# Products with rounded halves for the output and the state in an adaLN block, and bn_aggr in its first layer norm

## The chip, the cores and the metric

The kernel runs on one core of one Trainium2 chip. Its time is the device time of one execution in microseconds, here the median of three runs. Engines are called PE (TensorE), DVE (VectorE), ACT (ScalarE), POOL (GpSimd) and SP (SyncE, which issues the DMAs). Each works through its own list of instructions in order; semaphores tie the lists together.

## The reference

The input x is 16 batches of 512 positions with 256 channels. A block with adaptive layer norm is computed: a state space model and a gated mix, each behind a modulated layer norm and a gate.

```python
sa, ca, ga, sb, cb, gb = split((silu(c) @ wmod))      # per batch, 256 each
h = layernorm(x) * (1 + ca) + sa
u, gate = split(h @ W_in.T)
b_t = u @ W_state.T
dt = min(softplus(u @ W_dt.T + b_dt), 10)
decay = exp(-dt * rate)                                # rate from A_log
state[t] = decay[t] * state[t-1] + (1 - decay[t]) * b_t[t]    # 128 states
y = state @ W_C.T
z = y * silu(gate) + h * D
x = x + ga * (z @ W_out.T)
h = layernorm(x) * (1 + cb) + sb
xr, xk = mixes of h with h of the position before
out = x + gb * (sigmoid(xr @ W_r.T) * (relu(xk @ W_k.T)**2 @ W_v.T))
```

## The kernel before

A batch is worked in the layout channels x positions: two halves of 128 channels (partitions) by 512 positions. An fp32 array of this shape is 128x512 per half. The 16 batches run through a pipeline written out by hand: in step s each engine does parts of four batches, a = s, b = s-1, c = s-2 and d = s-3. Batch a gets its first layer norm (LN1) applied and transposed; b goes through the state space model (h, dt, b_t, gate, scan, y, z, W_out, x1); c through the second layer norm (LN2) and the mixes; d through W_k, W_r, W_v and the output. The order within a step is the order in the source of each engine's block; nothing reorders it. The four PSUM slots (of two banks each) are shared by several results, which sets more waits.

Most products are done in three passes. A value and its weight are each split into a rounded half of type fp32r (`_hi`) and the rest (`_lo` = value - hi, also fp32r). PE then adds hi x hi, hi x weight-lo and lo x weight-hi in PSUM: `half(out, w, at, x, c)` issues two products of 128x512 for half c of the input. ACT makes the hi parts (`nc.scalar.copy`), POOL the lo parts (`low_part`, L665). So it is for h, xk, xr and k. Two products are done in plain fp32: that of z with W_out (`half(o_out, w_late, OUT, z, ...)`, L207, four products a batch) and that of the state with W_C (L320, two a batch).

What touches the change, in the order of a step on each engine:

- PE: xk_hi of d, halves 0 and 1; dt, b_t of b from h_hi and xk_lo of d between them; dt from h_lo (ends dt, `dt_ps`); transposes of x1 of c (L290, `t2_ps`); xr_hi and the gate; y from the state of b (L320, `y_ps`); xr_lo half 0; half of the transposes of xn2 of c (L214); xr_lo half 1 (`r_ps`); the other transposes (`t3_ps`); k_hi; transposes of xn1 of a (L214, `t1_ps`); k_lo half 0; z half 0; k_lo half 1; z half 1 (`o_ps`).
- ACT: xk_hi, h, h_hi, xr_hi; the exp of dt (L427), relu, ln, decay; xn1 of a, tiles 0 and 1 (L446); k_hi (L452), silu (L456), k_act (L462); the tanh r_gate (L465, waits for `r_ps`); the four prevs of c (L392, wait for `t3_ps`), then the next step.
- DVE: the scan (L587, `state_ok`); xn2 (L526); y x silu (L599) and z (L604); xk, xr, xr, xk of c (L550, after `prev_ok`); LN1 statistics of batch a+2 (L489, bn_stats); rv (L624); LN1 mean and variance of a+2 (L496 to L505, five small instructions on 128x4); x2 of d (L631); x1 of b (L637, waits for `o_ps`); xn1 of a+1, tiles 2 and 3 (L520); the clip of dt (L644); LN2 statistics from `t2_ps` and its mean and variance; the drive (L658), which the scan follows.
- POOL: xk_lo, h_lo, xr_lo half 0; rstd of LN2 (L698); xr_lo half 1; LN1's rstd (L672, a pow) and shift (L674); k_lo.

x1 of batch b is made at the end of step s from PSUM, and PE transposes it in the next step. In the first two steps PE has idle stretches and runs products with zeros (`keep_warm`).

Of the kernel before, what the change touches and what calls it, by code (L numbers as in the profile page):

```python
# [26 lines left out]
def adaln_block(nc, x_tok_d, x_ch_d, w_d, wmod_d, c_d, cols_d, ident_d, out_d):  # L27
# [6 lines left out]
    with ExitStack() as ctx:  # L34
# [20 lines left out]
        wl_hi = sb("wl_hi", [P, CH, 3 * C], F32R)  # L55
        wl_lo = sb("wl_lo", [P, CH, 3 * C], F32R)
# [22 lines left out]
        mv1 = sb("mv1", [P, 2, 5, TT])  # L79
# [48 lines left out]
        wl_hi_ok, wl_lo_ok = sem("wl_hi_ok"), sem("wl_lo_ok")  # L128
# [74 lines left out]
        def _(pe):  # L203
# [43 lines left out]
            for s in STEPS:  # L247
                a, b, c, d = s, s - 1, s - 2, s - 3
                if live(d):
                    if d == 0:  # L250
# [4 lines left out]
                    half(k_out, wl_hi, MIX_K, xk_hi, 0, first=True)
                    half(k_out, wl_lo, MIX_K, xk_hi, 0)
                if live(d):
                    pe.wait_ge(xkhi_ok[1], d + 1)
# [50 lines left out]
                if live(b):  # L309
# [64 lines left out]
                if live(b):  # L374
# [4 lines left out]
        def _(act):  # L379
# [15 lines left out]
            for s in STEPS:  # L395
                a, b, c, d = s, s - 1, s - 2, s - 3
                if live(d):
# [68 lines left out]
                if live(c):  # L466
# [6 lines left out]
                    previous(REC, 0, c).then_inc(prev_ok[0], 1)  # L473
                    before(act, xr_ok[1], c)
# [5 lines left out]
        def _(dve):  # L480
# [11 lines left out]
            def mean_variance(st, mv, st_ok, halves_ok, spread_ok, mv_ok, k, negative=False):  # L492
# [6 lines left out]
                if negative:  # L499
                    nc.vector.scalar_tensor_tensor(mv[:, 0, :], mv[:, 2, :], 0.5, st[:, :, 1], ALU.mult, ALU.subtract)  # L500
                else:
                    nc.vector.scalar_tensor_tensor(mv[:, 0, :], mv[:, 2, :], -0.5, st[:, :, 1], ALU.mult, ALU.add)
# [79 lines left out]
            for s in STEPS:  # L582
                a, b, c, d = s, s - 1, s - 2, s - 3
                if live(b):
                    dve.wait_ge(drive_ok, b + 1)
                    before(dve, y_ps, b)
# [9 lines left out]
                if live(b):  # L596
# [5 lines left out]
                    for i in range(CH):  # L602
                        before(dve, o_ps, b)
# [57 lines left out]
        def _(pool):  # L661
# [5 lines left out]
            def ln1_scale(k):  # L667
# [81 lines left out]
```

## Time and profile before

| | |
|---|---|
| median of 3 runs | 390.41 us (390.02 to 390.94) |
| the profiled execution's own time | 390.1 us |
| its span in the trace | 388.3 us |
| PE, DVE, ACT, POOL busy | 95%, 82%, 74%, 52% of the span |

The profile is one execution. A line of a view in order of time has the start in us from the start of the span, the time it lasts, engine, source line, operation, output and inputs, and the count of instructions that were merged to it. A full fp32 product shows as two records. The start of a product on PE is when it was taken up, which can be a little before the one ahead has streamed through.

### The profile page before, as it was taken

The numbers are of one execution on the slowest core, as the hardware profiler recorded it, in microseconds if no ns is written. First come the engines' busy times: TensorE is split into PE (matmuls) and PEld (weight loads), VectorE is DVE, ScalarE is ACT, GpSimd is POOL, SyncE is SP. The second block draws the span as 40 slices with busy tenths as digits, with TensorE's granted clock in tenths as the row PEclk, the third lists the DMA queues.
The fourth block names the chain that finished last, engine by engine and source line by source line (L and its number), as shares of the span: only waits on it lengthen the run. The fifth ranks groups of instructions, "written<-read, shape, count | busy, mean of one in ns | idle before, by whom it ended". The sixth has DMA issues, their size and how long they took to land.

```text
span 388.3 us, 5293 instructions
## 1 busy us (share of the span) xinstructions
PE 369.3 (95%) x1624; PEld 265.3 (68%) x1627; DVE 317.1 (82%) x653; ACT 288.6 (74%) x375; POOL 201.8 (52%) x198
## 2 busy tenths in 40 slices
PE   8998899999999999999999999999999999999773
PEld 4766487676777677676767767676767767676651
DVE  3787987989889797988979798888979787768552
ACT  4467678687887878689687868888787878967471
POOL 2053355666364556656454566645455663635552
PEclk9999999999999999999999999999999999999998
DMA  8921111130403131040313113040302020000111
GB/s 283 394 77 54 54 57 54 56 110 0 164 0 108 55 104 60 12 152 0 118 47 108 56 56 107 3 159 3 111 0 87 24 92 17 23 32 0 57 54 54
DMA packets 18604, 29.13 MB, mean 75 GB/s; under 512 B 1168, under 2 KB 9616, under 8 KB 18448
## 3 DMA queue, kind: packets, MB, share of 16 engines
q1 hardware_dynamic: 18144, 28.71, 21.4%
q8 instruction: 13, 0.21, 0.2%
q10 hardware_dynamic: 432, 0.09, 0.1%
q14 instruction: 15, 0.12, 0.1%
HBM read 20.40 MB, written 8.39 MB: 74 GB/s over the span
## 4 chain that ended last, share of the span: by engine, by line
issue 49%; POOL 37%; PE 7%; DVE 3%; ACT 2%; POOLq 1%; DVEq 0%; ACTq 0%
POOL xr_lo L665 10%; POOL xk_lo L665 10%; POOL k_lo L665 6%; POOL h_lo L665 5%; POOL rstd L672 3%; PE slot L207 2%; PE slot L228 2%; PE slot L221 1%; DVE stats L489 1%; PE slot L320 1%; POOLq L24 1%; POOL prev L703 1%; PE slot L214 1%; ACT prev L392 1%; DVE state L587 1%
## 5 line engine op out<-in xcount | busy, mean ns | idle before, releaser
L665 POOL TENSOR_TENSOR xk_lo<-xk,xk_hi 128x512 fp32r<-128x512 f32 x32 | 40.9, 1279 | 52.7 <-ACT xk_hi L400 47.1
L207 PE MATMUL slot<-z,w_in 128*128 128x512 f32 x128 | 59.8, 592 | 0.0
L698 POOL TENSOR_TENSOR rstd<-mv,half_neg 128x4 f32<-128x4 f32 x16 | 16.1, 1007 | 76.5 <-DVE mv L505 76.5
L665 POOL TENSOR_TENSOR k_lo<-k_act,k_hi 128x512 fp32r<-128x512 f32 x32 | 40.6, 1291 | 20.7 <-ACT k_act L462 20.7
L392 ACT ACTIVATE prev<-slot,mod,mix_prev 128x512 f32<-128x512 f32 x64 | 44.5, 784 | 2.8 <-PE slot L214 2.8
L207 PE MATMUL slot<-h_hi,wf_hi 128*128 128x512 f32 x128 | 46.0, 400 | 0.4 <-ACT h_hi L415 0.4
L207 PE MATMUL slot<-h_hi,wf_lo 128*128 128x512 f32 x128 | 45.1, 393 | 0.0
L665 POOL TENSOR_TENSOR h_lo<-h,h_hi 128x512 fp32r<-128x512 f32 x30 | 38.3, 1298 | 9.6 <-ACT h_hi L415 9.6
L427 ACT ACTIVATE dt<-slot,cols 128x512 f32<-128x512 f32 x16 | 11.0, 688 | 41.5 <-PE slot L207 41.5
L665 POOL TENSOR_TENSOR xr_lo<-xr,xr_hi 128x512 fp32r<-128x512 f32 x32 | 41.5, 1299 | 0.0
L550 DVE SCALAR_TENSOR_TENSOR xk<-slot,mix_new,prev 128x512 f32<-128x512 f32 x32 | 23.9, 747 | 18.8 <-issue 18.8
L214 PE MATMUL slot<-ident,xn 128*128 128x128 f32 x256 | 35.7, 273 | 2.8 <-DVE xn L526 2.1
L207 PE MATMUL slot<-h_lo,wf_hi 128*128 128x512 f32 x128 | 37.4, 395 | 0.0
L214 PEld LDWEIGHTS slot<-ident,xn 128*128 128x128 f32 x256 | 30.4, 140 | 10.1 <-DVE xn L526 2.8
L207 PEld LDWEIGHTS slot<-z,w_in 128*128 128x128 f32 x128 | 24.0, 189 | 18.8 <-issue 16.3
L320 PE MATMUL slot<-state,w_in 128*128 128x512 f32 x64 | 30.2, 594 | 2.5 <-DVE state L587 2.5
L526 DVE TENSOR_SCALAR xn<-slot,mv,rstd 128x256 f32<-128x256 f32 x64 | 30.1, 534 | 1.1 <-POOL rstd L698 1.1
L599 DVE TENSOR_TENSOR slot<-silu,slot 128x1024 f32<-128x1024 f32 x16 | 19.7, 1229 | 13.5 <-PE slot L320 13.5
L465 ACT ACTIVATE r_gate<-slot 128x1024 f32<-128x1024 f32 x16 | 16.4, 1028 | 18.6 <-PE slot L207 18.6
L207 PEld LDWEIGHTS slot<-h_hi,wf_hi 128*128 128x128 f32 x128 | 24.0, 188 | 6.7 <-issue 0.9
L207 PE MATMUL slot<-xk_hi,wl_hi 128*128 128x512 f32 x64 | 26.2, 491 | 2.2 <-DVE xk L550 2.2
L207 PEld LDWEIGHTS slot<-h_hi,wf_lo 128*128 128x128 f32 x128 | 24.2, 189 | 5.9 <-issue 0.2
(99 smaller groups left out, 900.4 us busy)
## 6 DMA issues: line engine op xcount, KB each, us to landing
x_tok<-x_tok_in SPq DMA_DIRECT2D x16, 512.0 KB, 3.5
x_ch<-x_ch_in SPq DMA_DIRECT2D x16, 512.0 KB, 3.9
x_out<-wmod SPq DMA_DIRECT2D x15, 512.0 KB, 3.0
wmod<-wmod_in SPq DMA_DIRECT2D x1, 1024.0 KB, 10.1
w_in<-weights_in SPq DMA_DIRECT2D x1, 1024.0 KB, 11.5
w_in<-weights_in SPq DMA_DIRECT2D x1, 768.0 KB, 5.5
wmod<-wmod_in SPq DMA_DIRECT2D x1, 512.0 KB, 6.4
x_out<-wmod SPq DMA_DIRECT2D x2, 256.0 KB, 2.2
```

The costliest lines, as they stand in the source:

```text
L207: ins = nc.tensor.matmul(out, w[:, c, at + d * P:at + (d + 1) * P], x[:, c, :], start=first, stop=last)
L214: last = nc.tensor.transpose(out[:, c, t * P:(t + 1) * P], x[:, t, c * P:(c + 1) * P], ident[:])
L320: last = nc.tensor.matmul(ps_y[:, i, :], w_y[:, i * P:(i + 1) * P], state[:], start=True, stop=True)
L392: return nc.scalar.activation(prev[:, mix, i, 1:T + 1], ps_n[:, i, :], ACT.Identity, bias=mod_at(SHIFT2 + i, k), scale=mix_prev[:, mix, i, ...
L427: nc.scalar.activation(dt[:], ps_front[:, 0, :], ACT.Exp, bias=col(B_DT)).then_inc(e_ok, 1)
L465: nc.scalar.activation(r_gate[:], ps_r[:], ACT.Tanh, scale=0.5).then_inc(tanh_ok, 1)
L526: last = nc.vector.tensor_scalar(xn2[:, t, :], ps_x1[:, t, :], mv2[:, k % 2, 0, t:t + 1], rstd2[:, k % 2, t:t + 1], ALU.subtract, ALU.mult)
L550: nc.vector.scalar_tensor_tensor(x[:, i, :], ps_n[:, i, :], mix_now[:, mix, i, k:k + 1], prev[:, mix, i, 0:T], ALU.mult, ALU.add).then_inc ...
L599: nc.vector.tensor_tensor(ps_y[:], silu[:], ps_y[:], ALU.mult).then_inc(yg_ok, 1)
L665: nc.gpsimd.tensor_tensor(lo, x, hi.bitcast(F32), ALU.subtract).then_inc(done, 1)
L672: nc.gpsimd.tensor_tensor(rstd1[:, k % 2], mv1[:, k % 2, 1, :], half_neg[:], ALU.pow).then_inc(rstd1_ok, 1)
L698: nc.gpsimd.tensor_tensor(rstd2[:, c % 2], mv2[:, c % 2, 1, :], half_neg[:], ALU.pow).then_inc(rstd2_ok, 1)
```

## The change

The products of z with W_out and of the state with W_C are done with rounded halves in three passes from the third batch on (`WHOLE = 2`, `split(k)`); the first two batches keep the plain ones. For this W_out and W_C are split once in step 2 (b = 1) by ACT and POOL. In each step ACT makes state_hi (after xn1) and the two z_hi, POOL makes state_lo (after xr_lo half 1) and the two z_lo (after k_lo). PE does the hi parts where the product stood; the state's lo part comes after xr_lo half 0, and z's lo part in the next step, behind xk_hi half 0 and xk_hi half 1, where `o_ps` is now given. LN1's mean and variance on DVE are four `bn_aggr` instead of five small instructions, and two small `tensor_scalar` come to POOL before the pow. Its core:

```diff
@@ PE, step: c = s-2, d = s-3 @@
                     half(k_out, wl_hi, MIX_K, xk_hi, 0, first=True)
                     half(k_out, wl_lo, MIX_K, xk_hi, 0)
+                if split(c):
+                    pe.wait_ge(zlo_ok[0], c - WHOLE + 1)
+                    half(o_out, wl_hi, OUT, z_lo, 0)
                 if live(d):
                     pe.wait_ge(xkhi_ok[1], d + 1)
                     half(k_out, wl_hi, MIX_K, xk_hi, 1)
                     half(k_out, wl_lo, MIX_K, xk_hi, 1)
+                if split(c):
+                    pe.wait_ge(zlo_ok[1], c - WHOLE + 1)
+                    half(o_out, wl_hi, OUT, z_lo, 1, last=True).then_inc(o_ps, 1)
...
-                    pe.wait_ge(state_ok, b + 1)
-                    for i in range(CH):
-                        last = nc.tensor.matmul(ps_y[:, i, :], w_y[:, i * P:(i + 1) * P], state[:], start=True, stop=True)
-                    last.then_inc(y_ps, 1)
+                    if split(b):
+                        if b == WHOLE:
+                            pe.wait_ge(wy_lo_ok, 1)
+                        pe.wait_ge(shi_ok, b - WHOLE + 1)
+                        for i in range(CH):
+                            nc.tensor.matmul(ps_y[:, i, :], wy_hi[:, i * P:(i + 1) * P], state_hi[:], start=True, stop=False)
+                            nc.tensor.matmul(ps_y[:, i, :], wy_lo[:, i * P:(i + 1) * P], state_hi[:], start=False, stop=False)
+                    else:
...
                     half(r_out, wl_hi, MIX_R, xr_lo, 0)
+                if split(b):
+                    pe.wait_ge(slo_ok, b - WHOLE + 1)
+                    for i in range(CH):
+                        last = nc.tensor.matmul(ps_y[:, i, :], wy_hi[:, i * P:(i + 1) * P], state_lo[:], start=False, stop=True)
+                    last.then_inc(y_ps, 1)
...
-                    pe.wait_ge(z_ok[0], b + 1)
                     before(pe, tanh_ok, d + 1 if live(d) else 0)
-                    half(o_out, w_late, OUT, z, 0, first=True)
+                    if split(b):
+                        if b == WHOLE:
+                            pe.wait_ge(wl_lo_ok, 4)
+                        pe.wait_ge(zhi_ok[0], b - WHOLE + 1)
+                        half(o_out, wl_hi, OUT, z_hi, 0, first=True)
+                        half(o_out, wl_lo, OUT, z_hi, 0)
+                    else:
...
-                if live(b):
+                if split(b):
+                    pe.wait_ge(zhi_ok[1], b - WHOLE + 1)
+                    half(o_out, wl_hi, OUT, z_hi, 1)
+                    half(o_out, wl_lo, OUT, z_hi, 1)
+                elif live(b):
@@ ACT: start of a step; after xn1; in step 2; between the prevs @@
+                if split(c):
+                    act.wait_ge(z_ok[1], c + 1)
+                    nc.scalar.copy(z_hi[:, 1], z[:, 1]).then_inc(zhi_ok[1], 1)
...
+                if split(b):
+                    act.wait_ge(state_ok, b + 1)
+                    act.wait_ge(y_ps, b)
+                    nc.scalar.copy(state_hi[:], state[:]).then_inc(shi_ok, 1)
...
+                if b == 1:
+                    nc.scalar.copy(wl_hi[:, :, OUT:OUT + C], w_late[:, :, OUT:OUT + C]).then_inc(wl_hi_ok, 1)
+                    act.wait_ge(s_wy, 16)
+                    nc.scalar.copy(wy_hi[:], w_y).then_inc(wy_hi_ok, 1)
...
                     previous(REC, 0, c).then_inc(prev_ok[0], 1)
+                if split(b):
+                    act.wait_ge(z_ok[0], b + 1)
+                    before(act, o_ps, b)
+                    nc.scalar.copy(z_hi[:, 0], z[:, 0]).then_inc(zhi_ok[0], 1)
+                if live(c):
                     before(act, xr_ok[1], c)
                     previous(REC, 1, c)
@@ DVE: LN1; the scan and z wait for the low halves of the batch before instead of its product @@
             def ln1_mean_variance(k):
                 before(dve, shift1_ok, k - 1)
-                mean_variance(stats1[:, k % 2], mv1[:, k % 2], st1_ok, halves1_ok, spread1_ok, mv1_ok, k, negative=True)
+                dve.wait_ge(st1_ok, k + 1)
+                for t in range(TT):
+                    last = nc.vector.bn_aggr(mv1[:, k % 2, t, :], stats1[:, k % 2, t, :])
+                last.then_inc(mv1_ok, 1)
...
-                    before(dve, y_ps, b)
+                    if split(b - 1):
+                        dve.wait_ge(slo_ok, b - WHOLE)
+                    else:
+                        before(dve, y_ps, b)
...
-                        before(dve, o_ps, b)
+                        if split(b - 1):
+                            dve.wait_ge(zlo_ok[i], b - WHOLE)
+                        else:
+                            before(dve, o_ps, b)
@@ POOL: ln1_scale; after xr_lo half 1; after k_lo; in step 2 @@
-                nc.gpsimd.tensor_tensor(rstd1[:, k % 2], mv1[:, k % 2, 1, :], half_neg[:], ALU.pow).then_inc(rstd1_ok, 1)
+                nc.gpsimd.tensor_scalar(spread1[:, k % 2, 0, :], mv1[:, k % 2, :, 0], -1.0, None, ALU.mult)
+                nc.gpsimd.tensor_scalar(spread1[:, k % 2, 1, :], mv1[:, k % 2, :, 1], EPS, None, ALU.add).then_inc(spread1_ok, 1)
+                pool.wait_ge(spread1_ok, k + 1)
+                nc.gpsimd.tensor_tensor(rstd1[:, k % 2], spread1[:, k % 2, 1, :], half_neg[:], ALU.pow).then_inc(rstd1_ok, 1)
...
+                if split(b):
+                    pool.wait_ge(shi_ok, b - WHOLE + 1)
+                    pool.wait_ge(y_ps, b)
+                    nc.gpsimd.tensor_tensor(state_lo[:], state[:], state_hi[:].bitcast(F32), ALU.subtract).then_inc(slo_ok, 1)
                 if live(a + 1):
                     ln1_scale(a + 1)
...
+                if split(b):
+                    for i in range(CH):
+                        pool.wait_ge(zhi_ok[i], b - WHOLE + 1)
+                        pool.wait_ge(o_ps, b)
+                        nc.gpsimd.tensor_tensor(z_lo[:, i], z[:, i], z_hi[:, i].bitcast(F32), ALU.subtract).then_inc(zlo_ok[i], 1)
...
+                if b == 1:
+                    weight_low_part(4, OUT)
+                    pool.wait_ge(wy_hi_ok, 1)
+                    nc.gpsimd.tensor_tensor(wy_lo[:], w_y, wy_hi[:].bitcast(F32), ALU.subtract).then_inc(wy_lo_ok, 1)
```

## Rows read from the trace of the kernel before

**Rows 1.** The page, part 1: busy us (share of the span) xinstructions.
```profile
PE 369.3 (95%) x1624; PEld 265.3 (68%) x1627; DVE 317.1 (82%) x653; ACT 288.6 (74%) x375; POOL 201.8 (52%) x198
```

**Rows 2.** The table by stretches of time: one step, last step with b, tail.
```profile
200.00:222.26 22.26, 21.97 (x98) 15.92 (x97) 19.67 (x40) 17.80 (x24) 12.48 (x12) 1.00 0.21 72
...
327.00:348.20 21.20, 21.20 (x96) 15.70 (x95) 14.81 (x28) 16.60 (x21) 11.30 (x10) 1.00 0.07 26
...
348.20:388.30 40.10, 29.35 (x125) 20.65 (x123) 22.27 (x38) 20.68 (x27) 18.81 (x16) 0.96 0.11 40
```

**Rows 3.** PE in order of time: a step in the 200s, and the last one.
```profile
200.17 1.88 PE L207 MATMUL slot<-z,w_in 128*128 128x512 f32 x4
...
202.36 1.88 PE L207 MATMUL slot<-z,w_in 128*128 128x512 f32 x4
...
204.54 0.62 PE L207 MATMUL slot<-xk_hi,wl_lo 128*128 128x512 f32 x2
...
205.00 0.62 PE L207 MATMUL slot<-xk_hi,wl_hi 128*128 128x512 f32 x2
...
208.74 0.63 PE L207 MATMUL slot<-h_lo,wf_hi 128*128 128x512 f32 x2
...
209.66 1.09 PE L290 MATMUL slot<-ident,x 128*128 128x128 f32 x8 [0.29 <-DVE x L637]
...
215.71 1.88 PE L320 MATMUL slot<-state,w_in 128*128 128x512 f32 x4
...
341.76 0.63 PE L207 MATMUL slot<-h_lo,wf_hi 128*128 128x512 f32 x2
...
348.21 1.88 PE L320 MATMUL slot<-state,w_in 128*128 128x512 f32 x4
```

**Rows 4.** ACT in order of time, the same step.
```profile
209.40 0.69 ACT L427 ACTIVATE dt<-slot,cols 128x512 f32<-128x512 f32 x1 [2.64 <-PE slot L207]
...
213.59 1.09 ACT L446 ACTIVATE xn<-x_tok,shift,rstd 128x256 f32<-128x256 f32 x2
...
218.98 1.03 ACT L465 ACTIVATE r_gate<-slot 128x1024 f32<-128x1024 f32 x1 [1.11 <-PE slot L207]
...
219.90 2.78 ACT L392 ACTIVATE prev<-slot,mod,mix_prev 128x512 f32<-128x512 f32 x4
```

**Rows 5.** DVE in order of time, the same step.
```profile
201.82 1.39 DVE L489 BATCH_NORM_STATS2 stats<-x_tok 128x6 f32<-128x256 f32 x4
...
204.24 0.16 DVE L496 TENSOR_TENSOR mv<-stats 128x4 f32<-128x4 f32 x1
...
204.52 1.19 DVE L500 SCALAR_TENSOR_TENSOR mv<-mv,stats 128x4 f32<-128x4 f32 x1
...
206.89 1.40 DVE L631 SCALAR_TENSOR_TENSOR wmod<-slot,mod,x 128x512 f32<-128x512 f32 x2
...
213.67 1.22 DVE L587 TENSOR_TENSOR_SCAN state<-decay,slot 128x512 f32<-128x512 f32 x1
...
223.42 0.74 DVE L550 SCALAR_TENSOR_TENSOR xk<-slot,mix_new,prev 128x512 f32<-128x512 f32 x1
```

**Rows 6.** POOL in order of time, the same step.
```profile
204.39 2.56 POOL L665 TENSOR_TENSOR h_lo<-h,h_hi 128x512 fp32r<-128x512 f32 x2 [0.48 <-ACT h_hi L415]
...
215.47 1.01 POOL L672 TENSOR_TENSOR rstd<-mv,half_neg 128x4 f32<-128x4 f32 x1
...
216.56 0.20 POOL L674 TENSOR_TENSOR shift<-mv,rstd 128x4 f32<-128x4 f32 x1
```

**Rows 7.** DVE and POOL in order of time, step 3.
```profile
50.78 2.66 DVE L520 TENSOR_SCALAR xn<-x_tok,rstd,shift 128x256 f32<-128x256 f32 x2
...
51.95 1.34 POOL L665 TENSOR_TENSOR xr_lo<-xr,xr_hi 128x512 fp32r<-128x512 f32 x1
```

**Rows 8.** The tail, in order of time: x1 of the last batch.
```profile
359.16 1.40 DVE L637 SCALAR_TENSOR_TENSOR x<-slot,mod,x_ch 128x512 f32<-128x512 f32 x2
...
360.77 1.04 PE L290 MATMUL slot<-ident,x 128*128 128x128 f32 x8
```

More of the change, by code:

```diff
@@ L54, in adaln_block @@
         wf_lo = sb("wf_lo", [P, CH, 2 * NS + C], F32R)
-        wl_hi = sb("wl_hi", [P, CH, 3 * C], F32R)
-        wl_lo = sb("wl_lo", [P, CH, 3 * C], F32R)
+        wl_hi = sb("wl_hi", [P, CH, 4 * C], F32R)
+        wy_hi = sb("wy_hi", [P, C], F32R)
+        wy_lo = sb("wy_lo", [P, C], F32R)
+        wl_lo = sb("wl_lo", [P, CH, 4 * C], F32R)
         ident = sb("ident", [P, P])
@@ L78, in adaln_block @@
         stats1 = sb("stats1", [P, 2, TT, 6])
-        mv1 = sb("mv1", [P, 2, 5, TT])
+        mv1 = sb("mv1", [P, 2, TT, 2])
+        spread1 = sb("spread1", [P, 2, 2, TT])
         rstd1 = sb("rstd1", [P, 2, TT])
@@ L92, in adaln_block @@
         state = sb("state", [P, T])
+        state_hi = sb("state_hi", [P, T], F32R)
+        state_lo = sb("state_lo", [P, T], F32R)
         silu = sb("silu", [P, CH, T])
         z = sb("z", [P, CH, T])
+        z_hi = sb("z_hi", [P, CH, T], F32R)
+        z_lo = sb("z_lo", [P, CH, T], F32R)
         prev = sb("prev", [P, 2, CH, T + 1])
@@ L127, in adaln_block @@
         wsplit_hi, wsplit_lo = sem("wsplit_hi"), sem("wsplit_lo")
-        wl_hi_ok, wl_lo_ok = sem("wl_hi_ok"), sem("wl_lo_ok")
+        wl_hi_ok, wl_lo_ok, wy_hi_ok, wy_lo_ok = sem("wl_hi_ok"), sem("wl_lo_ok"), sem("wy_hi_ok"), sem("wy_lo_ok")
         mix_step, mix_ok = sem("mix_step"), sem("mix_ok")
@@ L156, in adaln_block, with split @@
         STEPS = range(0, NB + 4)
+        WHOLE = 2
+        def split(k):
+            return WHOLE <= k < NB
         block = ctx.enter_context(nc.Block())
@@ L317, in _ @@
                         pe.wait_ge(s_wy, 16)
-                    pe.wait_ge(state_ok, b + 1)
-                    for i in range(CH):
-                        last = nc.tensor.matmul(ps_y[:, i, :], w_y[:, i * P:(i + 1) * P], state[:], start=True, stop=True)
-                    last.then_inc(y_ps, 1)
+                    if split(b):
[6 more added lines that the diff above has]
+                    else:
+                        pe.wait_ge(state_ok, b + 1)
+                        for i in range(CH):
+                            last = nc.tensor.matmul(ps_y[:, i, :], w_y[:, i * P:(i + 1) * P], state[:], start=True, stop=True)
+                        last.then_inc(y_ps, 1)
                     if b == 0:
@@ L330, in _ @@
                     half(r_out, wl_hi, MIX_R, xr_lo, 0)
+                if split(b):
+                    pe.wait_ge(slo_ok, b - WHOLE + 1)
+                    for i in range(CH):
+                        last = nc.tensor.matmul(ps_y[:, i, :], wy_hi[:, i * P:(i + 1) * P], state_lo[:], start=False, stop=True)
+                    last.then_inc(y_ps, 1)
                 if live(c):
@@ L367, in _ @@
                         pe.wait_ge(s_wl, 16)
-                    pe.wait_ge(z_ok[0], b + 1)
                     before(pe, tanh_ok, d + 1 if live(d) else 0)
-                    half(o_out, w_late, OUT, z, 0, first=True)
+                    if split(b):
[5 more added lines that the diff above has]
+                    else:
+                        pe.wait_ge(z_ok[0], b + 1)
+                        half(o_out, w_late, OUT, z, 0, first=True)
                 if live(d):
@@ L490, in statistics, with mean_variance @@
                 last.then_inc(st_ok, 1)
-            def mean_variance(st, mv, st_ok, halves_ok, spread_ok, mv_ok, k, negative=False):
+            def mean_variance(st, mv, st_ok, halves_ok, spread_ok, mv_ok, k):
                 dve.wait_ge(st_ok, k + 1)
@@ L498, in mean_variance @@
                 dve.wait_ge(halves_ok, k + 1)
[L499 to L502, printed above, removed]
+                nc.vector.scalar_tensor_tensor(mv[:, 0, :], mv[:, 2, :], -0.5, st[:, :, 1], ALU.mult, ALU.add)
                 nc.vector.scalar_tensor_tensor(mv[:, 4, :], mv[:, 2, :], 0.25, mv[:, 2, :], ALU.mult, ALU.mult).then_inc(spread_ok, 1)
@@ L710, in _ @@
                         low_part(k_lo[:, i], k_act[:, i], k_hi[:, i], kact_ok, v_ps, klo_ok[i], d)
+                if split(b):
+                    for i in range(CH):
+                        pool.wait_ge(zhi_ok[i], b - WHOLE + 1)
+                        pool.wait_ge(o_ps, b)
+                        nc.gpsimd.tensor_tensor(z_lo[:, i], z[:, i], z_hi[:, i].bitcast(F32), ALU.subtract).then_inc(zlo_ok[i], 1)
                 if b == 0:
```

12 lines of the change are left out of this document (6 added, 6 removed).

## The prediction

> **What bounds the kernel now.** I read the page's busy table first: PE is busy for 95% of the span, DVE 82%, ACT 74%, POOL 52% [rows 1]. The table by stretches then shows the beat and the clock, 1.00 of full (the 2.4 GHz level) in the steps and 0.96 in the tail. A full step takes 22.26 us, and PE is busy for 21.97 us of it, so nearly all time between 60 and 327 us is PE's; the step without an LN1 part takes 21.20 us, and the last 40.1 us, after the last state product starts, are a tail in which PE is busy for 29.35 us only [rows 2].
>
> PE's order in time gives the prices [rows 3]. The starts 204.54 and 205.00 bracket two fp32r products: 0.465, so 0.2325 us for one of 512 columns. From 200.17 to 202.36 (2.19 us) PE does two full fp32 products of z and two fp32r ones of k_lo: (2.19 - 0.465) / 2 = 0.862 us for one fp32 product (its two records each; records start early in the queue, so I use only such closed intervals). PE has one real wait in a step, before the transposes of x1 at 209.66. From the start of the last dt product to the state product the stretch is 208.74 to 215.71, 6.97 us; the same work where x1 was early took 341.76 to 348.21, 6.45 us. So that wait costs 0.52 us a step.
>
> The other engines are not the bound but are close behind. ACT has no wait from the prevs at 219.90 to h_hi but 0.3 us for an xk; DVE and POOL have more room [rows 4 to 6].
>
> **The change, part by part.** I call T the start of the product of h_lo that ends dt (208.74 in the step shown).
>
> *W_out.* Four fp32 products, 4 x 0.862 = 3.45 us [rows 3], become twelve of fp32r, 12 x 0.2325 = 2.79: PE wins 0.66 us a batch. The last four of the twelve move behind xk_hi in the next step.
>
> *W_C.* Two of fp32, 1.72 us, become six, 1.40: 0.33 us won. The last two move behind xr_lo of half 0.
>
> All cost of the fp32 product is taken from rows. Beside it stands the Trainium skill, "FP8 and Floating Point Precision", section TensorE Precision Notes: true FP32 takes 4 passes. By that an fp32 product would be 0.93 and the two wins together 1.40 us a batch; the trace has 0.862, which is what decides.
>
> *x1 comes at another time.* DVE's LN1 arithmetic is five small instructions whose third starts at 204.52 and lasts 1.19 us; the set fills the time from 204.24 to 206.89, 2.65 us (the start of x2), because two of them wait out a POOL instruction. They become four bn_aggr. The trace has none. Bounds: 0.08 us, the spacing of the small instructions, and 1.25, one POOL instruction of waiting as for the one at 204.52 [rows 5, 6]. I take 0.1 to 0.2 each, 0.5 for four: it reads one array, as bn_stats does, and bn_stats (0.325 each) runs at 201.82 over POOL's xk_lo unstretched. So DVE gets 2.1 us back before x1. The Trainium skill, "SBUF — State Buffer", section Who interferes with whom, says that a DVE instruction with at most one SBUF input outside the 2-port modes does not contend with GpSimd; by it too the lower end would hold, but no row shows bn_aggr.
>
> *ACT* gets three casts of 128x512, 0.52 us each from start to start (a lone one is recorded as 0.62): state_hi before k_hi, z_hi[0] between the prevs, z_hi[1] before xk_hi. *POOL* gets three low parts of 1.255 us (two h_lo take 2.56 less the overlap) and two small tensor_scalars. For those the bounds are 0.2 us, the shift, and 1.0 us, the pow [rows 6]; I take 0.2, since they are no pows. *Once only*, ACT casts two more weight blocks (0.6 and 0.35 us) and POOL makes their low parts (1.3 and 0.65) in step 2, in idle time of both: cost nothing.
>
> **Do the new links hold?** With durations of the rows, all counted from T:
>
> PE could reach the state product at T+6.45. The exp of dt starts at T+0.66 (209.40 - 208.74) and lasts 0.69, and ACT is free behind the two xn1 tiles (213.59 + 1.0) at T+5.85 [rows 4]. On DVE the clip can start at T+1.42, and from clip to the scan's end all is one row of work: 0.34 for the clip, 1.5 for the LN2 statistics, 0.6 for their arithmetic, 0.73 for the drive, 1.22 for the scan [rows 5], with their hand-overs T+5.9. state_hi runs from there to T+6.6, so PE waits 0.15 us, and about 0.1 more to start anew (before, x1 was ready 0.41 us late and cost 0.52).
>
> One more thing comes before the clip. DVE's two xn1 instructions (L520) start in the step shown at 209.52 when POOL has just ended xr_lo, and cost 0.65. Where POOL was at work the same two took 2.66 us, from 50.78 to 53.44, the end of POOL's xr_lo (51.95 + 1.34) [rows 7]. After the change POOL has one low part and more to do before xk_lo: by the walk below its h_lo ends at T+20.7 and xr_lo[0] at T+22.0. L520 arrives near T+20.9, waits for xr_lo and ends at T+22.65; the clip, possible at 21.0 + 1.42, is 0.25 us late, and so are stats2, scan and state_hi: PE starts the state product near T+7.0 in all.
>
> From there PE has 22.26 - 6.97 - 0.99 = 14.30 us of work to the next T, if nothing on it waits. I walked it once with the state product at T+6.6 (what is later moves all of the following together). PE: y hi four products, xr_lo half 0, y lo (ready for it at T+8.0, done 8.5), four transposes of 0.11, xr_lo half 1 (r_ps T+9.55), four transposes, eight k_hi to 11.7, eight transposes, k_lo half 0, z_hi half 0 from 13.05, k_lo half 1, z_hi half 1 from 14.45, xk_hi from 15.35, z_lo, xk_hi, z_lo until 18.2, then dt, b_t and xk_lo up to 21.0. Against it:
> - state_lo: POOL's 1.3 us from T+6.65, there at 8.0, needed at 8.0.
> - ACT's row from r_ps: r_gate 0.92, two prevs of 0.66, z_hi[0] from 11.85, there at 12.5, needed at 13.05; two prevs; z_hi[1] from 13.7, at 14.35 against 14.45; xk_hi, h, xk_hi, h, h_hi (3.5 us) at 17.85 against 18.2.
> - xk: its last half needs the fourth prev, which z_hi[0] moves by 0.52; before, it started 4.44 us after r_gate (223.42 - 218.98 [rows 4, 5]), now 4.96, and is done at 15.3 against 15.35.
> - POOL: state_lo, LN1 scale to 9.9, k_lo to 12.4, z_lo[0] to 13.8, z_lo[1] behind z_hi[1] to 15.65, two xk_lo, two h_lo to 20.75 against 20.95.
> - DVE: xk done 15.3, statistics 1.3, rv 1.15, bn_aggr 0.5, x2 and x1 1.3 each: 20.9, and x1 is needed at 21.45, so the old wait of 0.52 is gone.
>
> Six links with 0 to 0.6 us to spare: I add 0.05 for those that miss.
>
> Step: 7.0 + 14.3 + 0.05 = 21.35 us, 0.91 less than 22.26.
>
> **The sum.** Between the state products of batches 2 and 15 lie twelve full steps and the short one. Up to batch 2 nothing changes but LN1. Twelve x 0.91 = 10.9. The short step has neither the x1 wait nor L520: 0.99 - 0.25 = 0.7. In the tail o_ps of the last batch comes later: before, x1 was done at 359.16 + 1.40 = 360.56, 12.35 us after the state product's start at 348.21, and its transposes ran from 360.77 (12.56) [rows 8]. Now W_out's last passes wait for z_hi[1] and the xk of batch 14, end 11.3 us after the state product's start, and two x1 instructions follow (1.4 us): 13.2 after it, 0.6 lost. Everything behind is one chain as before. Gain: 10.9 + 0.7 - 0.6 = 11.0 us. The profiled execution has 390.1 us (span 388.3), so 379.1; the median of 390.41 is 0.3 above it: **379.3 us**.
>
> **The rivals.**
>
> *A, forecast:* 377 to 382.5, with a step of 21.2 to 21.6. Chance 0.50.
>
> *B, no port wait:* L520 finds POOL idle, or the clip has air. Then the state product starts at T+6.7, the step is 21.0: 12 x 1.26 + 0.7 - 0.6 = 15.2 us, about 375. For it: the margin of 0.25 is small. Against: POOL works without a break from T+12.6 to T+22. Chance 0.20, 373.5 to 377.
>
> *C, POOL's row is too long:* if each small tensor_scalar costs 1.0 as the pow does, shift ends 1.6 us later, k_lo[1] at 13.95, z_lo[1] at 16.5, h_lo at T+21.55, 0.6 after PE wants it, and xr_lo[0] then holds L520 0.5 longer. Step 22.1 to 22.2: gain 2 us, 388. It decides from some 0.5 us each on; half of it gives 384. Chance 0.17 for 382.5 to 389.6. That the gain is eaten up within 0.2% is the edge of this: 0.05.
>
> *D, slower:* bn_aggr waits for POOL as the instruction at 204.52 does. POOL has no gap there any more, so four of them end with POOL's instructions at T+18.2, 19.45, 20.7 and 22.0, x1 at 24.7 instead of before 21.4: 3.3 us more a step, 24.6 us, 13 x 2.4 = 31 us slower, 421. The turning point is at one to two of the four waiting (x1 1.5 us late). Against it: bn_stats over xk_lo. Chance 0.08.
>
> **How the numbers follow.** About 0.2% (0.8 us) is what a measurement here can tell from no change. Faster: A + B + C = 0.87; same 0.05; slower 0.08. Leaving out D, the null and the tip of B and C gives 374 to 386.5 for 8 in 10; the likeliest case alone is 377 to 382.5.
>
> **What would show it.** In the profile after: between 80 and 320 us the state products 21.35 us apart; no z or state product in plain fp32 but for two batches; no PE wait on x1, a small one on state_hi (ACT) at the state product; bn_aggr near 0.15 us; L520's pair over 1.2 us, ending with POOL's xr_lo; POOL unbroken from k_lo to xr_lo. It would be wrong if PE waits for xk, z_lo or h_lo by some tenths in each step, if fp32r products at 0.2325 us can't be kept up with their weights changing every time, or if bn_aggr is long.

## The result and the profile after

The changed kernel takes 377.76 us (median of 4 runs, 377.76 to 377.79) against 390.43 us before: a ratio of 0.9675, 95% interval 0.9658 to 0.9692, 12.7 us less. The prediction was 379.3 us with a step of 21.35 us. The profiled execution has a span of 375.9 us (388.3 before), and the ratios below are against executions of the kernel before on the same chip.

The page's busy table after, and the table by stretches for one step, the tail, and the eleven steps between the state products of batches 2 and 13 (for the first three, the rows of before are in [rows 1, 2]). A line by stretches has the window, its length, the busy us of PE, PEld (PE's weight loads), DVE, ACT and POOL, the granted clock, the DMA share and GB/s.

```profile
PE 359.1 (96%) x1708; PEld 276.4 (74%) x1711; DVE 302.0 (80%) x637; ACT 308.8 (82%) x419; POOL 265.6 (71%) x274
...
201.09:222.27 21.18, 21.18 (x103) 16.74 (x102) 18.44 (x39) 19.16 (x26) 16.86 (x18) 1.00 0.23 75
...
334.83:375.90 41.07, 29.34 (x131) 21.40 (x130) 22.38 (x38) 22.52 (x30) 22.65 (x19) 0.97 0.10 39
...
59.37:292.40 233.03, 233.03 (x1124) 184.29 (x1123) 202.73 (x419) 210.78 (x287) 185.28 (x188) 1.00 0.22 73
```

The same eleven steps before:

```profile
59.88:304.72 244.84, 241.65 (x1058) 175.08 (x1056) 216.49 (x431) 196.17 (x254) 137.43 (x133) 1.00 0.20 69
```

A step is 233.03 / 11 = 21.18 us against 22.26, at a granted clock of 1.00 in both. PE's records cover the whole of it. ACT and POOL have grown, as the casts and low parts want it; DVE has shrunk.

PE in order of time, one step after, from T (201.09, the product of h_lo that ends dt) to the next T [rows 3]:

```profile
201.09 0.62 PE L220 MATMUL slot<-h_lo,wf_hi 128*128 128x512 f32 x2
201.56 1.03 PE L309 MATMUL slot<-ident,x 128*128 128x128 f32 x8
...
206.63 1.09 PE L220 MATMUL slot<-h_lo,wf_hi 128*128 128x512 f32 x4
207.62 0.50 PE L342 MATMUL slot<-state_hi,wy_hi 128*128 128x512 f32 x1
...
208.19 0.39 PE L342 MATMUL slot<-state_hi,wy_hi 128*128 128x512 f32 x1
...
215.09 0.62 PE L220 MATMUL slot<-k_lo,wl_hi 128*128 128x512 f32 x2
215.55 0.69 PE L220 MATMUL slot<-z_hi,wl_hi 128*128 128x512 f32 x2
...
217.60 0.63 PE L220 MATMUL slot<-z_lo,wl_hi 128*128 128x512 f32 x2
...
222.27 0.62 PE L220 MATMUL slot<-h_lo,wf_hi 128*128 128x512 f32 x2
```

The transposes of x1 at 201.56 have no wait any more. Two small losses are hidden in the spacings, though PE's records leave no gap. From 206.63 to 208.19 there are six products, 6 x 0.2325 = 1.40, and it takes 1.56: 0.16 us lost at the state product. From 215.09 to 217.60 there are ten, 2.33, and it takes 2.51: 0.19 lost at z_hi half 1 and xk_hi. The trace has reasons for both parts of the second: the weights of z_hi half 1 are loaded at 215.50, when ACT has just ended that z_hi (214.81 + 0.64), and those of xk_hi at 216.57, just behind DVE's last xk (215.64 + 0.74), which reads the PSUM slot that these products write.

DVE, ACT and POOL in order of time around the end of the step [rows 4 to 6]:

```profile
218.74 0.37 DVE L571 BATCH_NORM_AGGREGATE mv<-stats 128x2 f32<-128x6 f32 x4
219.03 1.37 DVE L696 SCALAR_TENSOR_TENSOR wmod<-slot,mod,x 128x512 f32<-128x512 f32 x2
220.32 1.40 DVE L702 SCALAR_TENSOR_TENSOR x<-slot,mod,x_ch 128x512 f32<-128x512 f32 x2
221.64 1.70 DVE L579 TENSOR_SCALAR xn<-x_tok,rstd,shift 128x256 f32<-128x256 f32 x2
223.65 0.43 DVE L709 TENSOR_SCALAR dt<-dt 128x512 f32<-128x512 f32 x1 [0.31 <-ACT dt L473]
```
```profile
206.95 0.62 ACT L498 CAST state_hi<-state 128x512 fp32r<-128x512 f32 x1
```
```profile
209.03 0.23 POOL L737 TENSOR_SCALAR spread<-mv 128x4 f32<-128x4 f32 x1
...
213.67 1.30 POOL L787 TENSOR_TENSOR z_lo<-z,z_hi 128x512 fp32r<-128x512 f32 x1 [0.22 <-ACT z_hi L531]
215.53 1.30 POOL L787 TENSOR_TENSOR z_lo<-z,z_hi 128x512 fp32r<-128x512 f32 x1 [0.56 <-ACT z_hi L442]
216.79 2.55 POOL L730 TENSOR_TENSOR xk_lo<-xk,xk_hi 128x512 fp32r<-128x512 f32 x2
219.29 2.55 POOL L730 TENSOR_TENSOR h_lo<-h,h_hi 128x512 fp32r<-128x512 f32 x2
221.79 1.40 POOL L730 TENSOR_TENSOR xr_lo<-xr,xr_hi 128x512 fp32r<-128x512 f32 x1
```

The four bn_aggr (L571) take 0.29 us from their first start to x2's (L696), all of it under POOL's back-to-back low parts. The two xn1 instructions (L579) do wait for POOL, which is what the prediction calls the port wait: the pair takes 1.70 us instead of the 0.72 before and 0.79 in apply_late below, where POOL does not hold it up. But the clip of dt (L709) behind them still waits 0.31 us for ACT.

**The ledger.** Start to state product of batch 2: 59.88 to 59.37, 0.51 us won. Eleven full steps: 11.81. The two steps after them: 43.49 us (304.72 to 348.21) to 42.43 (292.40 to 334.83), 1.06. Tail: 40.09 to 41.07, 0.98 lost. Sum 12.40, the difference of the spans.

Of the 0.51 at the start, 0.34 lies before the first state product (21.82 to 21.48), a stretch that scatters from 21.23 to 21.88 in the traces of kernels that are alike up to there. The first step is 0.35 shorter, as in the others with bn_aggr. The second is 0.18 longer, which it is not in aggr_only and out_only, where batch 2's product has no state_hi to wait for.

### The profile page after: what moved, and what is told of

Same layout as the page of the kernel before. It is cut to its first block, busy times and chain, and to the rows that moved or that the text cites. A ratio compares the mean times of both kernels' runs of the same rounds, so it can differ in the third digit from the quotient of the medians.

```text
span 375.9 us, 5636 instructions
## 1 busy us (share of the span) xinstructions
PE 359.1 (96%) x1708; PEld 276.4 (74%) x1711; DVE 302.0 (80%) x637; ACT 308.8 (82%) x419; POOL 265.6 (71%) x274
## 4 chain that ended last, share of the span: by engine, by line
POOL 47%; issue 39%; PE 5%; DVE 3%; ACT 2%; DMA 1%; POOLq 1%; DVEq 0%; SPq 0%; ACTq 0%
POOL xr_lo L730 11%; POOL z_lo L787 7%; POOL xk_lo L730 6%; POOL k_lo L730 6%; POOL h_lo L730 6%; POOL state_lo L777 5%; POOL rstd L740 3%; PE slot L220 2%; DMA w_in<-weights_in 1%; PE slot L234 1%; PE slot L347 1%; DVE stats L548 1%; POOL prev L771 1%; POOL spread L738 1%; POOL spread L737 1%
## 5 line engine op out<-in xcount | busy, mean ns | idle before, releaser
L435 ACT ACTIVATE prev<-slot,mod,mix_prev 128x512 f32<-128x512 f32 x64 | 46.3, 786 | 1.7 <-PE slot L227 1.7
L787 POOL TENSOR_TENSOR z_lo<-z,z_hi 128x512 fp32r<-128x512 f32 x28 | 36.2, 1294 | 12.0 <-ACT z_hi L442 7.9
L730 POOL TENSOR_TENSOR xr_lo<-xr,xr_hi 128x512 fp32r<-128x512 f32 x32 | 42.5, 1331 | 0.0
L227 PEld LDWEIGHTS slot<-ident,xn 128*128 128x128 f32 x256 | 29.5, 141 | 11.4 <-issue 4.9
L661 DVE TENSOR_TENSOR slot<-silu,slot 128x1024 f32<-128x1024 f32 x16 | 19.7, 1229 | 16.9 <-PE slot L361 15.4
L220 PEld LDWEIGHTS slot<-h_lo,wf_hi 128*128 128x128 f32 x128 | 24.0, 189 | 6.0 <-issue 0.4
L609 DVE SCALAR_TENSOR_TENSOR xr<-slot,mix_new,prev 128x512 f32<-128x512 f32 x32 | 23.7, 746 | 5.5 <-ACT prev L435 5.5
L579 DVE TENSOR_SCALAR xn<-x_tok,rstd,shift 128x256 f32<-128x256 f32 x32 | 25.1, 827 | 1.9 <-POOL shift L742 1.9
L702 DVE SCALAR_TENSOR_TENSOR x<-slot,mod,x_ch 128x512 f32<-128x512 f32 x32 | 22.5, 744 | 4.0 <-PE slot L220 4.0
```

Source lines behind the costliest of these rows:

```text
L220: ins = nc.tensor.matmul(out, w[:, c, at + d * P:at + (d + 1) * P], x[:, c, :], start=first, stop=last)
L227: last = nc.tensor.transpose(out[:, c, t * P:(t + 1) * P], x[:, t, c * P:(c + 1) * P], ident[:])
L435: return nc.scalar.activation(prev[:, mix, i, 1:T + 1], ps_n[:, i, :], ACT.Identity, bias=mod_at(SHIFT2 + i, k), scale=mix_prev[:, mix, i, ...
L579: last = nc.vector.tensor_scalar(xn1[:, t, :], x_tok[:, k % 3, t, :], rstd1[:, k % 2, t:t + 1], shift1[:, k % 2, t:t + 1], ALU.mult, ALU.add)
L609: nc.vector.scalar_tensor_tensor(x[:, i, :], ps_n[:, i, :], mix_now[:, mix, i, k:k + 1], prev[:, mix, i, 0:T], ALU.mult, ALU.add).then_inc ...
L661: nc.vector.tensor_tensor(ps_y[:], silu[:], ps_y[:], ALU.mult).then_inc(yg_ok, 1)
```

## The experiments

"Step" is the spacing of the state products in the trace, in us, in the middle of the run.

| run | what differs | us | step |
|---|---|---|---|
| before | | 390.4 | 22.26 |
| after | | 377.8 | 21.18 |
| aggr_only | no product split | 384.4 | 21.75 |
| splits_only | old LN1 arithmetic | 406.2 | 22.83 to 26.99 |
| out_only | W_C plain | 380.3 | 21.31 |
| state_only | W_out plain | 382.7 | 21.62 |
| pow1, pow2 | 1, 2 more pows on POOL | 378.0, 391.1 | 21.18, 21.94 |
| apply_late | L579 elsewhere | 377.6 | 21.18 |
| last_whole | last W_out plain | 376.3 | 21.18 |
| shi_soon | state_hi sooner | 379.4 | 21.32 |
| zhi_dve | z_hi[0] from DVE | 382.0 | 21.48 |
| best | last_whole, shi_soon and zhi_dve together | 377.5 | 21.32 |
| silu_first | shi_soon, last_whole, silu first | 373.1 | 20.96 |

**The parts alone.** aggr_only makes split() False throughout and keeps LN1's bn_aggr and POOL's two small instructions; splits_only is the changed kernel with this put back:

```diff
-                dve.wait_ge(st1_ok, k + 1)
-                for t in range(TT):
-                    last = nc.vector.bn_aggr(mv1[:, k % 2, t, :], stats1[:, k % 2, t, :])
-                last.then_inc(mv1_ok, 1)
+                mean_variance(stats1[:, k % 2], mv1[:, k % 2], st1_ok, halves1_ok, spread1_ok, mv1_ok, k, negative=True)
```

> The LN1 aggregations and POOL's two small instructions alone, all products as before. Theory: DVE comes to x1 2.3 us sooner in each full step, PE's wait before the transposes of x1 (0.52 us) goes, the full step becomes 21.74 us as the last two steps of the kernel before were; 11 full steps give 5.7 us and the start 0.5: 384.2 us. Rival: the whole gain is that of the products, and the aggregations only move idle time of DVE: 390 us.

> Both product splits with the old five-instruction LN1 arithmetic on DVE. Theory: POOL is now busy all through that arithmetic, two to three of its instructions wait out one POOL instruction each, it ends 1.7 us or more later than bn_aggr, x1 comes 0.6 us or more late and PE waits again: a step of 22.0 us, 387 us (385 to 390), so that the two parts are worth more together than one by one. Rival: x1 has room enough, PE sets the step with its shorter work: 378 to 380 us.

aggr_only came as expected: 384.35 us (ratio 0.9839, 0.9814 to 0.9864), each step 21.75 us, the two last ones too. splits_only did not: 406.19 us, ratio 1.040 (1.034 to 1.047), slower than before by 16 us, where 387 was expected. The direction of the theory holds, its size was far off. DVE, POOL and PE of splits_only in order of time, in a step of the worse kind, with PE's wait of the commoner kind (217.65) behind:

```profile
186.10 0.62 DVE L554 TENSOR_TENSOR mv<-stats 128x4 f32<-128x4 f32 x1
186.64 1.33 DVE L555 SCALAR_TENSOR_TENSOR mv<-stats 128x4 f32<-128x4 f32 x1
188.00 1.23 DVE L558 SCALAR_TENSOR_TENSOR mv<-mv,stats 128x4 f32<-128x4 f32 x1
189.15 1.31 DVE L561 SCALAR_TENSOR_TENSOR mv<-mv 128x4 f32<-128x4 f32 x1
190.50 0.16 DVE L563 SCALAR_TENSOR_TENSOR mv<-mv 128x4 f32<-128x4 f32 x1
```
```profile
184.14 2.56 POOL L729 TENSOR_TENSOR xk_lo<-xk,xk_hi 128x512 fp32r<-128x512 f32 x2
186.65 2.56 POOL L729 TENSOR_TENSOR h_lo<-h,h_hi 128x512 fp32r<-128x512 f32 x2
189.16 1.29 POOL L729 TENSOR_TENSOR xr_lo<-xr,xr_hi 128x512 fp32r<-128x512 f32 x1
```
```profile
193.37 1.97 PE L308 MATMUL slot<-ident,x 128*128 128x128 f32 x8 [3.11 <-DVE x L701]
...
217.65 1.09 PE L308 MATMUL slot<-ident,x 128*128 128x128 f32 x8 [1.67 <-DVE x L701]
```

These instructions work on four numbers a partition, and one after the other gets its turn only when a POOL instruction ends (186.64 + 1.33, 188.00 + 1.23 and 189.15 + 1.31 end with POOL's two h_lo and its xr_lo). The same set in the commoner step:

```profile
211.83 0.62 DVE L554 TENSOR_TENSOR mv<-stats 128x4 f32<-128x4 f32 x1
212.37 0.15 DVE L555 SCALAR_TENSOR_TENSOR mv<-stats 128x4 f32<-128x4 f32 x1
212.56 1.15 DVE L558 SCALAR_TENSOR_TENSOR mv<-mv,stats 128x4 f32<-128x4 f32 x1
213.63 0.15 DVE L561 SCALAR_TENSOR_TENSOR mv<-mv 128x4 f32<-128x4 f32 x1
213.81 1.15 DVE L563 SCALAR_TENSOR_TENSOR mv<-mv 128x4 f32<-128x4 f32 x1
```

Here the second and the fourth slip in behind the one ahead without a wait, so the set takes 3.05 us against 4.5 in the worse step; four bn_aggr take 0.29. What decides between the two kinds is not shown. PE idles 1.67 us for x1 in the commoner step, which is then 22.84 us. In the worse one it idles 3.11 us, and behind that the granted clock is lower; the table by stretches of splits_only:

```profile
194.00:195.00 1.00, 1.00 (x8) 1.00 (x6) 0.29 (x1) 0.64 (x2) 0.00 (x0) 0.50 0.77 219
...
197.00:198.00 1.00, 1.00 (x6) 0.82 (x5) 0.93 (x6) 0.99 (x3) 0.30 (x1) 1.00 0.00 0
```

0.50 is the 1.2 GHz level. Three of the eleven full steps are of this kind (25.75, 25.80, 26.99 us). The first of them is 2.91 us longer than a commoner one: 1.44 is the longer idle time, and 1.47 is PE's busy time, 22.64 us instead of 21.17 at a mean granted clock of 0.93. Of the 16.9 us that the eleven steps lose against before, these three account for 11.8. The expectation had x1 0.6 us late and nothing of the clock. The two steps without LN1 arithmetic are 21.02 and 21.17. The parts are thus not additive: 6 us won, 16 lost, together 12.7 won.

**One product at a time.** split(k) is taken apart into split_y for the state and split_z for z; out_only has split_y False throughout, state_only split_z.

> After, but the state's product stays in plain fp32 (no state_hi, no state_lo). Theory: PE loses 0.33 us a batch and saves the 0.19 that it now loses at the state product: step 21.3 us, 379.5 us. Rival: each split is worth its own PE saving: 14 x 0.33 more than after, 382.4 us.

> After, but z's product stays in plain fp32. Theory: PE's step is 21.74 - 0.33 + 0.19 at the state product, 21.6 us, and the tail is as before: 382.3 us. Rival: without the z_hi casts nothing else is late, and the wait at the state product goes too: 21.4 us, 380 us.

Both steps came as the first theory had them: 21.31 and 21.62 us. The medians are 380.29 (0.9733, 0.9708 to 0.9759), 0.8 above the expected, and 382.65 (0.9801, 0.9779 to 0.9824). W_C's split is worth 21.31 - 21.18 = 0.13 us a step of its 0.33, since PE loses 0.16 at state_hi; W_out's is worth 21.62 - 21.18 = 0.44 of its 0.66, with 0.19 lost at z_hi half 1 and xk_hi. The two add up: 0.57, as from aggr_only's 21.75 to 21.18.

**POOL's room.** An unused pow of 128x4 stands once or twice before the shift.

```diff
+                for n in range(1):
+                    nc.gpsimd.tensor_tensor(waste[:, k % 2, n], spread1[:, k % 2, 1, :], half_neg[:], ALU.pow)
                 pool.wait_ge(rstd1_ok, k + 1)
                 nc.gpsimd.tensor_tensor(shift1[:, k % 2], spread1[:, k % 2, 0, :], rstd1[:, k % 2], ALU.mult).then_inc(shift1_ok, 1)
```

> After, with one more pow of 128x4 (its result unused) on POOL in each LN1 scale: what the prediction's rival C asked, POOL's row 1.0 us longer. Theory from the trace after: POOL has waits of 0.22 and 0.56 us at the two z_lo and h_lo comes some 0.2 us before PE wants it, so the time stays within 1 us of 377.8. Rival: POOL's row is the bound with no room, 13 x 1.0 more: 390 us.

> After, with two more pows a step. Theory: the waits are used up, h_lo is 0.9 us late in each of 12 steps: 388 us (386 to 390). Rival: POOL still has room, 378 us.

pow1: 378.02 us (0.9675, 0.9630 to 0.9719), step 21.18: 1.0 us more on POOL costs nothing. pow2: 391.09 us (1.0027, 1.0003 to 1.0052), step 21.94; it gives back the whole gain. The turning point lies between. 12 x 0.76 = 9 us of it are the steps; 4.2 us more were lost before the state product of batch 2 (63.60 against 59.37), which the expectation left out. PE of pow2, in order of time:

```profile
201.59 0.74 PE L221 MATMUL slot<-k_lo,wl_hi 128*128 128x512 f32 x2 [0.21 <-POOL k_lo L731]
...
210.48 0.71 PE L221 MATMUL slot<-h_lo,wf_hi 128*128 128x512 f32 x2 [0.22 <-POOL h_lo L731]
```

PE waits for POOL at two places and not only at h_lo. With PE later there, the 0.19 at z_hi half 1 and xk_hi is gone in this run (k_lo at 203.10 to z_lo at 205.44, ten products, 2.34 us), though ACT's order is the old one.

**The port wait before the clip.** ln1_apply goes behind ln2_apply of the next step.

```diff
                     ln2_apply(c, range(TT // 2, TT), xn2b_ok)
+                if live(a) and a > 2:
+                    ln1_apply(a)
...
-                if live(a + 1) and a > 0:
+                if live(a + 1) and a == 1:
                     ln1_apply(a + 1)
```

> After, with DVE's two xn1 instructions (L579) of a batch moved from before the clip of dt to behind the xn2 instructions of the next step, into DVE's wait for y_ps. Theory from the trace after: the port wait of 1.0 us at these instructions has cover, as the clip still waits 0.31 us for ACT's exp; no change, 377.8 within 0.5. Rival, the prediction's own term: the port wait costs 0.25 us a step on the way to the state, 12 x 0.25: 374.8 us.

377.55 us (0.9665, 0.9628 to 0.9702), step 21.18: no change. DVE of this run, in order of time:

```profile
202.26 0.43 DVE L711 TENSOR_SCALAR dt<-dt 128x512 f32<-128x512 f32 x1 [1.93 <-ACT dt L473]
...
208.41 0.79 DVE L579 TENSOR_SCALAR xn<-x_tok,rstd,shift 128x256 f32<-128x256 f32 x2
```

The pair's 1.70 us have become 0.79, and the clip waits 1.93 us for ACT instead of 0.31: the port wait was real, and covered.

**The tail.** W_out is split for batches 2 to 14 only.

> After, but W_out of the last batch in plain fp32. Theory: in the tail PE is not the bound, o_ps of the last batch comes sooner when its passes do not stand behind xk_hi and z_lo; the tail goes back from 41.1 to 40.1 us: 376.8 us. Rival: the tail is longer for the state's split or for something else: 377.8 us or more.

376.33 us (0.9638, 0.9599 to 0.9676); the tail from the last state product is 39.9 us instead of 41.1. The transposes of the last x1, after and in last_whole:

```profile
348.35 1.09 PE L309 MATMUL slot<-ident,x 128*128 128x128 f32 x8 [0.57 <-DVE x L702]
```
```profile
346.76 1.03 PE L312 MATMUL slot<-ident,x 128*128 128x128 f32 x8
```

They start 13.52 us behind the last state product after (334.83) and 12.32 in last_whole (334.44), against 12.56 before; from there to the end it is 27.5 us in all three traces. So the tail's loss is that of o_ps behind other work.

**PE's two small losses.** shi_soon takes LN2's arithmetic to bn_aggr and puts state_hi between ACT's two xn1 tiles; zhi_dve computes z_hi half 0 on DVE, and PE and ACT wait for it before they overwrite what it reads.

```diff
                     for t in range(TT // 2):
+                        if t == 1:
+                            state_high()
                         last = nc.scalar.activation(xn1[:, t, :], x_tok[:, a % 3, t, :], ACT.Identity,
```
```diff
+                    if split(b):
+                        before(dve, o_ps, b)
+                        nc.vector.scalar_tensor_tensor(z_hi[:, 0, :], h[:, b % 2, 0, :], col(D0), ps_y[:, 0, :], ALU.mult, ALU.add).then_inc(zhi_ok[0], 1)
```

> After, with the way to state_hi cut on both of its engines: LN2's arithmetic on DVE is four bn_aggr too (POOL adds the epsilon), and ACT makes state_hi between its two xn1 tiles. Theory: state_hi comes 0.35 us sooner, PE's loss of 0.19 us at the state product goes in each of 13 steps: 375.4 us. Rival: the next link (silu for the transposes of xn2, or state_lo) is as late, and nothing is won: 377.8 us.

> After, with z_hi of half 0 computed by DVE a second time from PSUM instead of cast by ACT between the prevs. Theory: the fourth prev, the last xk and z_hi of half 1 come 0.52 us sooner; PE's losses at z_hi half 1 and at xk_hi, 0.2 us a step, go: 375.2 us. Rival: PE loses this time for another reason (the pace of the products themselves) or DVE becomes late with x1: 377.8 us or more.

> The two changes of shi_soon and zhi_dve and the plain W_out for the last batch together. Theory: PE without a wait needs 20.75 us a step; 13 x 0.43 and 1.0 of the tail: 371.5 us. Rival: the links share their slack, one of the two losses stays: 374 us.

All three missed. shi_soon and best came out slower than even their rivals had it; zhi_dve lies in its rival's "377.8 us or more", but for a cause that the rival does not name. PE of shi_soon, then of zhi_dve, in order of time:

```profile
207.99 0.39 PE L343 MATMUL slot<-state_hi,wy_hi 128*128 128x512 f32 x1
...
210.22 0.63 PE L228 MATMUL slot<-ident,xn 128*128 128x128 f32 x4 [0.16 <-ACT silu L514]
```
```profile
215.50 1.06 PE L227 MATMUL slot<-ident,xn 128*128 128x128 f32 x8 [0.30 <-DVE z_hi L671]
```

In shi_soon the loss at the state product is gone (207.99 follows the four products that start at 207.05 by 0.94), but silu has become late by more, and the transposes of xn2 wait for it: step 21.32, 379.38 us (0.9725, 0.9707 to 0.9743). Its rival named this link and had it cost as much as was won. In zhi_dve the products of z_hi and xk_hi run at full pace, but z_hi is a third reader of the PSUM bank that xn1's transposes are written to next, and they wait for it, 0.46 us by the spacing; the expectation had not looked at the bank. Step 21.48, 382.04 us (0.9796, 0.9775 to 0.9817). Since PE comes to z_hi half 1 later here, as it does in pow2, the run does not tell whether moving z_hi[0] would have taken the 0.19 away by itself. best is 377.46 us (0.9671, 0.9656 to 0.9685), step 21.32, with silu's wait as in shi_soon: the tail's gain pays for the slower step.

silu_first drops zhi_dve, keeps shi_soon and last_whole and moves ACT's silu ahead of k_hi.

> shi_soon with ACT's silu moved ahead of k_hi, and W_out of the last batch in plain fp32. shi_soon took PE's loss at the state product away and got a wait for silu before the transposes of xn2, since silu ended 0.37 us later against PE. Theory: with silu first both are gone, k_hi has 1 us of room; step 21.0 us instead of 21.18 (12 full steps and one more: 2.3 us) and the tail 1.2 to 1.4 us shorter as in last_whole: 374.0 us. Rival: silu now waits for the gate product itself and r_gate or k_lo comes late, the step stays at 21.2 to 21.3 and only the tail is won: 376.3 us or more.

373.11 us (5 runs, 372.99 to 373.44), ratio 0.9558, 0.9541 to 0.9575: faster than both kernels, 4.6 us under the changed one. ACT and PE of this run, in order of time:

```profile
205.06 0.60 ACT L505 ACTIVATE xn<-x_tok,shift,rstd 128x256 f32<-128x256 f32 x1
205.63 1.03 ACT L513 ACTIVATE silu<-slot 128x1024 f32<-128x1024 f32 x1
206.56 1.05 ACT L517 ACTIVATE k_hi<-k_act 128x1024 fp32r<-128x1024 f32 x1
```
```profile
204.50 1.10 PE L224 MATMUL slot<-h_lo,wf_hi 128*128 128x512 f32 x4
205.43 0.40 PE L346 MATMUL slot<-state_hi,wy_hi 128*128 128x512 f32 x1
...
205.90 0.39 PE L346 MATMUL slot<-state_hi,wy_hi 128*128 128x512 f32 x1
```

Six products from 204.50 to 205.90 in 1.40 us, nothing lost; a step is 20.96. The 0.19 at z_hi half 1 and xk_hi stays (212.79 to 215.31 for ten products), and 20.96 less that is 20.77, next to the 20.75 of the step without any wait. Of the 5.0 us between the spans of the changed kernel and this one, 3.0 are the thirteen steps, 1.4 the tail and 0.6 the start.

## Why the prediction came true, and where its sizes were off

The time is right, and so is the main mechanism (points 1 and 2). That it lies in forecast A's range is in part luck: A's port wait did not cost anything, which is rival B's second condition ("or the clip has air"), and links that A had at 0.05 us cost 0.19. The step, 21.18, lies between A's 21.2 and B's 21.0.

1. *PE sets the step, and the products cost what the rows say.* Right. fp32r products whose weights change every time keep their pace of 0.2325 us, and the wins of 0.66 and 0.33 us are there once the losses are counted (points 4, 5 and silu_first). The Trainium skill's rule of 4 passes ("FP8 and Floating Point Precision", TensorE Precision Notes), at 0.2325 us a pass, would have made it 1.40 us a batch, an estimate. The trace's 0.862 us for an fp32 product is four times 0.2155, and it leaves 0.99. PE's total work of 20.75 us a step (21.74 without the x1 wait, less 0.99) fits the measured 21.18 less its losses of 0.35.
2. *x1's wait of 0.52 us goes, by bn_aggr.* Right, and shown alone by aggr_only: 22.26 to 21.75. bn_aggr's 0.29 us for four is below the 0.5 taken. None of the four waits for POOL, as the prediction had argued from bn_stats.
3. *Port wait of 0.25 us before the clip.* Wrong, and this is the term that failed: "L520 arrives near T+20.9, waits for xr_lo and ends at T+22.65". It arrived 0.63 us before the next T (221.64), so one of its two instructions slipped in before xr_lo and stretched that (1.40 instead of 1.29); the pair ended 1.07 after T instead of 1.65, and the clip had 0.31 to spare. apply_late shows the cost to be nothing. POOL's row was not unbroken either: it waits 0.22 and 0.56 us before the two z_lo.
4. *Wait for state_hi, 0.25 us.* Measured 0.16. The scan ends at 206.91 and ACT starts state_hi at 206.95, right behind xn1, as walked.
5. *Links between T+7 and T, 0.05 us.* Measured 0.19, at z_hi half 1 and xk_hi. The links are those named: z_hi[1] from ACT, and xk behind the fourth prev. That z_hi[0] between the prevs makes them late is argued from ACT's row, which runs from the first prev to z_hi[1] without a gap (211.64 to 215.45); no run shows it by itself, since in zhi_dve and pow2 PE comes later too.
6. Points 3 to 5 sum to 0.55 us predicted (0.6 with the rounding to T+7.0) and 0.35 measured, on top of 20.75 (the prediction's own floor, 6.45 + 14.30); 0.08 us of the measured step I could not place. Step 21.35 against 21.18.
7. *Twelve full steps and a short one.* A misreading: the stretch that begins at 327.00 [rows 2] cut 0.5 us off its step. The kernel before has eleven steps of 22.26 and two of 21.75. Taking one short step for a full one is worth 0.91 - 0.74, some 0.2 us, so the miscount hardly shows in the time: 10.9 + 0.7 foreseen, 11.81 + 1.06 measured, and the difference is the step's.
8. *Start:* 0.51 us in the two traces, which the prediction counted as nothing; only the 0.35 of the first step is LN1's for certain. *Tail:* 0.98 lost instead of 0.6, and by the mechanism named (last_whole). The prediction's sum there does not close (11.3 + 1.4 is 12.7, not 13.2). Measured, W_out's last pass ends 12.0 us after the state product and x1 is done 13.5 after it. Together: steps 1.3 us better than foreseen, start 0.5, tail 0.4 worse, which is the 1.4 from 11.0 to 12.4.
9. *Rival C* (POOL's row too long): the small tensor_scalars are 0.23 us and not 1.0, and its turning point was set too low: "some 0.5 us each" is 0.6 more in all, but pow1 has 1.0 more for nothing, and in pow2 2.0 more cost 0.76 a step.
10. *Rival D* was priced for the wrong instruction. bn_aggr does not wait, but the kernel with the splits and without bn_aggr is what D describes: small DVE instructions chained to POOL's, x1 late, slower than before.

## What to carry to other kernels

Work moved to GpSimd has a second price beside its own time: VectorE instructions under it can wait until the running GpSimd instruction ends, however small they are. Here it was those with two SBUF inputs (0.15 us became 1.15 to 1.33) and the tensor_scalar from SBUF to SBUF (L579), but not bn_stats, bn_aggr or those that read one input from PSUM. Look for them first, and replace them before GpSimd's idle time is filled. Two edits that look unrelated can then be worth nothing, or less, without each other. When several in-order engines are within tenths of the bound, walk the links in the new order, PSUM bank releases included, and expect a repair of one link to show the next one.

## What the runs showed of the hardware that I had not expected

- Of the chain of five small DVE instructions of 128x4, 0.15 to 0.17 us each when POOL is idle, three in a row lasted 1.23 to 1.33 us each, in step with POOL's low parts (186.64 to 190.46 in splits_only).
- After 3.11 us of idle PE the granted clock was 0.50 at 194 to 196 us and 1.00 again from 197; after 1.67 us of idle it stayed at 1.00 (the step from 200.85 to 223.69).
- A product whose input is ready just in time cost PE 0.16 us at state_hi and 0.19 at z_hi half 1 and xk_hi together, though PE's row has no wait there: look at the spacing of the starts, not at the idle column. With state_hi 0.3 us sooner (shi_soon, silu_first) the 0.16 was gone.
